# Expert stage of a fused kernel: five batches' rows scattered by expert and worked off in 95 tiles

## The reference, cut to what matters

```python
h = (x - mean) / sqrt(var + eps)
scores = sigmoid(h @ Wg.T)                       # 16 a row
choice = scores + bias                           # 4 groups of 4; the best 2 groups by
                                                 # the sum of their best two; then the best 4
w = scores[top4] / (sum(scores[top4]) + 1e-20) * 2.5
shared = relu2(h @ Ws1.T) @ Ws2.T                # 256 -> 256 -> 256, relu2(v) = relu(v)^2
x = x + shared + sum over the 4 chosen e of w_e * (relu2(h @ W1[e].T) @ W2[e].T)   # 256 -> 128 -> 256
```

## Time and profile before

| | us |
|---|---|
| median of 3 runs | 3248.0 (3244.1 to 3249.63) |
| the profiled execution | 3243.28 |
| its span, first to last instruction | 3241.4 |
| StageE, from its first load to the end of the span | 2688.0 to 3241.4 |

### The profile page before, as it was taken

One profiled execution on the slowest core, in us unless ns is written; L12 is line 12 of the kernel. 1 busy time (PEld: TensorE's weight loads), 2 busy tenths in 40 slices (PEclk: granted clock), 3 DMA queues, 4 the chain that ended last, 5 costly groups with the idle time before them and its releaser, 6 DMA issues.

```text
span 3241.4 us, 40482 instructions
## 1 busy us (share of the span) xinstructions
PE 2788.6 (86%) x13782; PEld 1680.9 (52%) x13782; DVE 2130.8 (66%) x3827; ACT 1629.6 (50%) x2433; POOL 1030.1 (32%) x715
## 2 busy tenths in 40 slices
PE   6878878887765799999969999968888988999999
PEld 3445544554443455555535666534444445666666
DVE  0688898888895677777522222246777785777776
ACT  2778778777861355555431111148877781111111
POOL 0888888888781221121010000011111000110000
PEclk9899999999867899999979999979999998999999
DMA  3577887788773775555432000010000002000000
GB/s 106 118 169 148 179 172 168 147 180 172 161 169 81 192 184 90 93 81 91 54 133 67 23 23 23 19 49 7 7 7 14 1 1 59 7 14 7 7 7 13
DMA packets 119272, 262.94 MB, mean 81 GB/s; under 512 B 14784, under 2 KB 72896, under 8 KB 117408
## 3 DMA queue, kind: packets, MB, share of 16 engines
q0 software_dynamic: 24928, 134.89, 20.0%
q1 hardware_dynamic: 94144, 125.47, 16.9%
HBM read 135.40 MB, written 131.20 MB: 82 GB/s over the span
## 4 chain that ended last, share of the span: by engine, by line
PE 50%; issue 6%; ACT 6%; DVE 5%; DMA 1%; SPq 0%; POOL 0%; POOLq 0%; ACTq 0%; DVEq 0%
PE PS L2345 7%; PE PS L1625 6%; PE PS L2363 6%; PE PS L1916 4%; PE PS L1647 3%; PE PS L1288 2%; PE PS L1966 2%; ACT Z L2074 2%; PE PS L1245 2%; PE PS L1267 2%; PE PS L1924 2%; PE PS L1270 2%; PE PS L1215 2%; PE PS L1984 1%; PE PS L1314 1%
## 5 line engine op out<-in xcount | busy, mean ns | idle before, releaser
L804 POOL TENSOR_TENSOR Z<-Z 128x1024 f32<-128x1024 f32 x256 | 648.4, 2761 | 45.8 <-DMA Z<-rows_b 40.9
L714 DVE TENSOR_TENSOR_SCAN Z<-PS,Z 128x1024 f32<-128x1024 f32 x256 | 576.5, 2276 | 18.4 <-POOL Z L804 13.6
L508 PE MATMUL PS<-Z 128*128 128x128 f32 x2048 | 305.1, 295 | 121.3 <-DVE Z L714 47.6
L508 PEld LDWEIGHTS PS<-Z 128*128 128x128 f32 x2048 | 250.7, 151 | 252.6 <-issue 81.7
L646 ACT ACTIVATE PS<-Z 128x511 f32<-128x511 f32 x512 | 332.8, 688 | 68.2 <-DVE Z L714 67.6
L1384 ACT ACTIVATE Z<-PS 128x512 f32<-128x512 f32 x320 | 188.9, 596 | 266.7 <-PE PS L1270 261.4
L2396 ACT ACTIVATE Z<-PS 128x512 f32<-128x512 f32 x144 | 85.9, 597 | 415.4 <-PE PS L2345 415.4
L2345 PE MATMUL PS<-Z 128*128 128x512 f32 x576 | 275.3, 604 | 7.9 <-DVE Z L2478 7.1
L658 ACT ACTIVATE Z<-PS,Z 128x512 f32<-128x512 f32 x378 | 246.0, 684 | 68.3 <-PE PS L508 61.5
L1477 DVE TENSOR_REDUCE Z<-PS 128x1 f32<-128x512 f32 (+2 forms) x384 | 182.8, 508 | 120.2 <-PE PS L1246 116.6
L2074 ACT ACTIVATE Z<-Z 128x2048 f32<-128x2048 f32 x128 | 252.4, 1996 | 12.9 <-PE PS L1966 9.3
(11 more groups left out here) (289 smaller groups left out, 4959.9 us busy)
## 6 DMA issues: line engine op xcount, KB each, us to landing
sums<-Z POOLq DMA_DIRECT2D x112, 768.0 KB, 8.4
Z<-rows_b SPq DMA_DIRECT2D x128, 256.0 KB, 4.6
Z<-scr SPq DMA_DIRECT2D x256, 128.0 KB, 7.2
rows_n<-in_L_ffn_expert_wv POOLq DMA_DIRECT2D x32, 528.0 KB, 7.7
scr<-Z SPq DMA_DIRECT2D x32, 384.0 KB, 3.5
Z<-Z POOLq DMA_DIRECT2D x14, 768.0 KB, 7.6
Z<-in_L_ffn_expert_wv SPq DMA_DIRECT2D x4, 2048.0 KB, 15.0
Z<-sums SPq DMA_DIRECT2D x7, 768.0 KB, 6.3
```

The costliest lines, as they stand in the source:

```text
L508: ins = e.transpose(self.turned[i % 2][:, c * 128:(c + 1) * 128], self.h(k, c // 2)[:, c % 2, i * 128:(i + 1) * 128], ident)
L714: e.tensor_tensor_scan(h, a, h, 0.0, ALU.mult, ALU.add).then_inc(s["scan"], 1)
L804: e.tensor_tensor(self.h(k, f), self.du[b % 2][:, 2 * f:2 * f + 2, :], b3(self.Bs[k % 2], 1, [128, 2, 512]), ALU.mult).then_inc(s["hin"], 1)
```

## The change

Batches 0 to 4 (`SP = 5`) no longer go through all experts. For each, DVE ranks the scores as before, POOL's part of it now on DVE too (`choice`), PE counts by matmuls with a triangular and an all-ones matrix how many rows before this one chose the same expert (`prefix`), DVE works out from that each row's four places (`place`), and POOL scatters the batch's normalised rows with 16 indirect DMAs of 128 rows (`rows_out`) into `rows_e`, a DRAM tensor with a region of 2,688 rows for each expert. That tensor is filled with finite numbers during StageD, by 32 DMAs from DRAM to DRAM on SP's queue, each behind a `yf` step. `slots` then works out, for each of 95 places (80 full tiles' worth of rows, and at most 15 more for the remainders of 16 experts), its expert and where it starts. Meanwhile PE does the shared expert and the first six experts (`FIRST = 6`) of batch 5.

Then come **95 tiles**: a gather of 128 rows (POOL), two transposes (`head`), a copy (ACT), the expert's number and two 128-column multiplications (`ups`), relu (ACT) and product (DVE), a transpose (`flips`) and a copy (DVE), one 256-column multiplication (`downs`), a copy (ACT) and a store to `rows_ye` (SP). Between them lie the preparation of batches 6 and 7 and `posy`, the places in `rows_ye`. Last, the ten remaining experts of batch 5 and batches 6 and 7 go through all experts as before; between their `down` steps, 20 `back` steps each gather four times 128 rows from `rows_ye` (POOL), and add them with their weights to x (DVE). The diff, cut to its core:

```diff
+        self.rows_e = m.nc.dram_tensor("rows_e", [StageE.NE * StageE.REG, 256], F32, kind="Internal").ap()
+        self.d_fill = m.lasting("d_fill_e")
...
+        n = StageE.NE * StageE.REG // StageE.FILLS
+        some = d["L0_ffn_expert_wv"].rearrange("x k m -> (x k m)")[0:n * 256].rearrange("(p n) -> p n", p=112)
+        for i in range(StageE.FILLS):
+            e.wait_ge(s["yf"], i + 1)
+            e.dma_start(self.rows_e[n * i:n * (i + 1)].rearrange("(p n) c -> p (n c)", p=112), some).then_inc(self.d_fill, 16)
...
+    SP, NE = 5, 16
+    NS = 16 * SP + NE - 1
+    REG = 128 * (4 * SP + 1)
+    FILLS = 32
+
+    FIRST = 6
...
+        def ahead(b):
+            return [("stats", b), ("rstd", b)], [("minus", b), ("norm", b), ("flip", b, 0), ("flip", b, 1), ("flipped", b),
+                                                 ("logits", b), ("exp", b)]
+
+        def shared(b):
+            return [("hidden", b, 0), ("hidden", b, 1)], [("down", b, 0, 0), ("down", b, 0, 1)]
+
+        def experts(b, xs):
+            out = []
+            for x in xs:
+                if x + 2 < 16:
+                    out.append(("hidden", b, x + 4))
+                out += [("down", b, 1 + x, 0), ("down", b, 1 + x, 1)]
+            return out
+
...
+        for b in range(2):
+            out += [s for part in ahead(b) for s in part]
+        for b in range(SP):
+            first, then = shared(b)
+            out += [("choice", b), *first, ("prefix", b)]
+            if b + 2 <= SP:
+                out += ahead(b + 2)[0]
+            out += [("place", b), ("rows_out", b)]
+            out += then
+            if b + 2 <= SP:
+                out += ahead(b + 2)[1]
+        first, then = shared(SP)
+        out += [("slots",), ("choice", SP), *first, ("hidden", SP, 2), *then, ("hidden", SP, 3)]
+        out += experts(SP, range(self.FIRST))
+        late = []
+        for b in range(SP + 1, NB):
+            late += ahead(b)[0] + ahead(b)[1] + [("choice", b)]
+        late = [("posy",)] + late
+        at = 0
+        out += [("head", 0), ("head", 1)]
+        for c in range(-1, NS + 1):
+            for what, i in (("ups", c + 1), ("rows", c + 4), ("head", c + 2), ("flips", c), ("downs", c - 1)):
+                if what == "head" and i < 2 or what == "rows" and i < 4:
+                    continue
+                if 0 <= i < NS:
+                    out.append((what, i))
+            upto = len(late) if c >= NS - 20 else len(late) * (c + 1) // (NS - 20)
+            out += late[at:upto]
+            at = upto
+        out += experts(SP, range(self.FIRST, 16))
+        for b in range(SP + 1, NB):
+            first, then = shared(b)
+            out += first + [("hidden", b, 2)] + then + [("hidden", b, 3)] + experts(b, range(16))
+
+        n = out.index(("down", SP, 1 + self.FIRST, 0))
+        downs = [i for i in range(n, len(out)) if out[i][0] == "down"]
+        every = max(1, len(downs) * 4 // 5 // (4 * SP))
+        where = {downs[every * g + 2]: g for g in range(4 * SP)}
+        full = []
+        for i, s in enumerate(out):
+            full.append(s)
+            if i in where:
+                b, k = divmod(where[i], 4)
+                full.append(("back", b, k))
+        return full
...
+        def head(c):
+            e.wait_ge(*self.d_gr.done(c))
+            if c >= 2:
+                e.wait_ge(s["hs"], c - 1)
+            else:
+                e.wait_ge(s["hid"], self.ups_before)
+            for k in range(2):
+                ins = e.transpose(self.hb[c % 2][:, k * 128:(k + 1) * 128], self.gr[c % 4][:, k * 128:(k + 1) * 128], ident)
+            ins.then_inc(s["ht"], 1)
+
+        def ups(c):
+            e.wait_ge(s["hs"], c + 1)
+            if c == 0:
+                e.wait_ge(s["slot"], 1)
+                e.wait_ge(s["acc"], self.dns_before)
+                for g in range(4):
+                    e.wait_ge(self.d_e[g], 32)
+            if c >= 2:
+                e.wait_ge(s["af"], c - 1)
+            expert[c] = e.value_load(self.esi[0:1, c:c + 1], min_val=0, max_val=self.NE - 1)
+            for k in range(2):
+                ins = e.matmul(self.ub[c % 2], self.hs[c % 2][:, k, :],
+                               self.w1f[:, bass.ds(expert[c] * 256 + 128 * k, 128)], start=k == 0, stop=k == 1)
+            ins.then_inc(s["tu"], 1)
+
+        def flips(c):
+            e.wait_ge(s["th"], c + 1)
+            e.transpose(self.tbk[c % 2], self.th[c % 2], ident).then_inc(s["flp"], 1)
+
+        def downs(c):
+            e.wait_ge(s["af"], c + 1)
+            if c >= 2:
+                e.wait_ge(s["y"], c - 1)
+            e.matmul(self.db[c % 2][:, 0:256], self.af[c % 2], self.w2f[:, bass.ds(expert[c] * 256, 256)],
+                     start=True, stop=True).then_inc(s["td"], 1)
+
...
+        def head(c):
+            e.wait_ge(s["ht"], c + 1)
+            if c >= 2:
+                e.wait_ge(s["tu"], c - 1)
+            e.activation(self.hs[c % 2].rearrange(FLAT), self.hb[c % 2][:, 0:256], ACT.Copy).then_inc(s["hs"], 1)
+
+        def ups(c):
+            e.wait_ge(s["tu"], c + 1)
+            if c >= 2:
+                e.wait_ge(s["th"], c - 1)
+            e.activation(self.tr[c % 2], self.ub[c % 2], ACT.Relu).then_inc(s["tr"], 1)
+
+        def downs(c):
+            e.wait_ge(s["td"], c + 1)
+            if c >= 3:
+                e.wait_ge(self.d_y[c % 3], 16 * (c // 3))
+            e.activation(self.yo[c % 3], self.db[c % 2][:, 0:256], ACT.Copy).then_inc(s["y"], 1)
+
...
+        def slots_(*_):
...
+            e.wait_ge(*own.now())
+            e.tensor_reduce(tiles, self.cmp, AX.X, ALU.add).then_inc(*own.tick())
+            for x in range(16):
                 e.wait_ge(*own.now())
-                e.reciprocal(sc, sc).then_inc(*own.tick())
+                e.tensor_tensor(tb[:, x + 1:x + 2], tb[:, x:x + 1], tiles[:, x:x + 1], ALU.add).then_inc(*own.tick())
+            e.wait_ge(*own.now())
+            shape = [128, NS, 15]
+            e.tensor_tensor(past, b3(slots, 2, shape), b3(tb[:, 1:16], 1, shape), ALU.is_ge).then_inc(*own.tick())
...
+            e.tensor_tensor(past, past, b3(tiles[:, 0:15], 1, shape), ALU.mult).then_inc(*own.tick())
+            e.wait_ge(*own.now())
+            e.tensor_reduce(loc, past, AX.X, ALU.add).then_inc(*own.tick())
+            e.tensor_copy(self.esi, es)
+            e.wait_ge(*own.now())
+            e.tensor_tensor(loc, slots, loc, ALU.subtract).then_inc(*own.tick())
+            e.wait_ge(*own.now())
+            e.tensor_scalar(loc, loc, float(4 * SP), 128.0, ALU.min, ALU.mult)
...
+        def ups(c):
+            e.wait_ge(s["tr"], c + 1)
+            if c >= 2:
+                e.wait_ge(s["flp"], c - 1)
+            e.tensor_tensor(self.th[c % 2], self.tr[c % 2], self.ub[c % 2], ALU.mult).then_inc(s["th"], 1)
+
+        def flips(c):
+            e.wait_ge(s["flp"], c + 1)
+            if c >= 2:
+                e.wait_ge(s["td"], c - 1)
+            e.tensor_copy(self.af[c % 2], self.tbk[c % 2]).then_inc(s["af"], 1)
+
+        def back(b, k):
+            for t in range(4):
+                g = 16 * b + 4 * k + t
+                e.wait_ge(self.d_gy[g % 8], 16 * (g // 8 + 1))
+                e.wait_ge(*((s["gat"], g - 3) if k else (s["acc"], self.n_dn[b, 0, t // 2] + 1)))
+                xx = m.X[:, 4 * b + t, :]
+                w = 16 * b + 4 * t + k
+                e.scalar_tensor_tensor(xx, self.gy[g % 8], self.wk[:, w:w + 1], xx, ALU.mult, ALU.add).then_inc(s["gat"], 1)
+
+        self.walk(stats=stats, minus=minus, choice=choice, place=place, slots=slots_, posy=posy, hidden=hidden, down=down,
+                  ups=ups, flips=flips, back=back)
...
+        def rows_out(b):
+            e.wait_ge(s["posi"], b + 1)
+            if b == 0:
+                e.wait_ge(self.d_fill, 16 * self.FILLS)
+            for t in range(4):
+                for k in range(4):
+                    c = 16 * b + 4 * t + k
+                    e.indirect_dma_start(self.rows_n, bass.IndirectOffsetOnAxis(ap=self.posi[:, c:c + 1], axis=0),
+                                         self.nt[b][:, t, :], None).then_inc(self.d_rows, 16)
+
+        def rows(c):
+            if c >= 4:
+                e.wait_ge(s["ht"], c - 3)
+            e.indirect_dma_start(self.gr[c % 4], None, self.rows_n,
+                                 bass.IndirectOffsetOnAxis(ap=self.start[:, c:c + 1], axis=0)).then_inc(*self.d_gr.over(c))
+
+        def head(c):
+            if c == 0:
+                e.wait_ge(s["slot"], 1)
+                e.wait_ge(self.d_rows, 256 * self.SP)
+                for i in range(4):
+                    rows(i)
+
+        def back(b, k):
+            if (b, k) == (0, 0):
+                e.wait_ge(s["posy"], 1)
+                for i in range(3):
+                    e.wait_ge(self.d_y[i], 16 * len(range(i, NS, 3)))
+            for t in range(4):
+                g, c = 16 * b + 4 * k + t, 16 * b + 4 * t + k
+                if g >= 8:
```

(88 more changed lines are left out.)

398 lines of the change are left out of this document (233 added, 165 removed).

## The result

The changed kernel takes 3321.3 us, median of 4 runs (3312.4 to 3340.1), against 3248.8 before (median of 4 runs, one more than above): ratio 1.0228, 95% interval 1.0200 to 1.0256. The forecast was 3301 us and slower; the time lies 20 us above it, inside its own range (3275 to 3325) and inside the wide one (3238 to 3352). It also lies nearer to the numbers of two rivals, 3334 for the half clock and 3324 for the bound by gathers, than to the forecast's.

The account below looks back on a forecast made before the run. PE was taken to bound StageE; seven steps summed to 606.2 us against 553.4, +52.8, giving span 3294.2 and median 3301 us, 1.6% slower. Its own range was 3275 to 3325, 8 in 10 3238 to 3352.

Parts of the forecast that it names:

- the half clock: Rival: PE's half clock holds through the tiles, 2.75 us a tile, 33 us more, 3334 us; chance 0.17.
- the bound by gathers: Rival: gathers of `back` become the bound, 4 x 1.57 us against 5.17, 23 us more, 3324 us; chance 0.09.
- Steps 1 to 4: StageE ahead of the tiles: first choice 13 us, five batches 108, `slots` and batch 5's choice 24.7, cover for scatters 32.
- a shared `down` at half clock: In the five batches: shared `down` at half clock outlasts DVE's moments and `place`, 1.6 us more a batch.
- Step 5: The 95 tiles: 228 us at 2.4 a tile, 32 for work put in between, 5 lead and drain; 265 us.
- The work put into the ring: In the tiles: two choices, `posy`, norms, flips and scores on DVE, and the clock after stalls; together 32 us.
- the ring: In the tiles: up product, relu, product, DVE's copy, then the load behind that wait; 2.32 us a turn, taken as 2.4.
- The faster rival: Load costs nothing or DVE's copy comes in time: tiles at 1.3 to 1.5 us, 90 us less, 3211 us; chance 0.16.
- Its deciding point: In the tiles: the rival of faster tiles decides from 1.85 us a tile down.
- Step 6: After the tiles, the rest through all experts: 155 us plus 4 for late first gathers, 159 us; returns barely fit.
- Step 7 and StageD: Last matmul to end 4.5 us, as now; fills in StageD 0, at most 5 if a gather is late.

Follow-up runs that it names:

- e5: Changed kernel plus four extra transposes a tile on PE, ahead of its `downs`, that nobody reads: 3340.0 us, ratio 1.0285.
- e12: Changed kernel with only the load of the expert's number moved ahead of both waits of the up product, on chip 3: 3282.9 us, ratio 1.0096.
- e10: Kernel of e8 without the 80 gathers of result rows and their 80 additions, on chip 3: 3223.3 us, ratio 0.9917.
- e4: Kernel before, with nothing of the change but its 32 fills in StageD: 3242.3 us, ratio 0.9985.
- e6: The changed kernel, unaltered, run again on chip 2: 3318.6 us, ratio 1.0215 to the kernel before.
- e7: Changed kernel with the load ahead of both waits of the up product and the flips' results in another bank: 3223.0 us, ratio 0.9921.
- e8: As e7, with the two late choices and `posy` cut into single instructions laid between tiles: 3205.8 us, ratio 0.9862.

## Why the prediction was right, and where it was 20 us off

Against the first profile after. StageE lasted 628.6 us where 606.2 were predicted.

The span missed by 30 us (3324.6 for 3294.2) and the median by 20. The 10 between are luck: the prediction put the median 4.7 us above the profiled execution, and it lay 5.1 below.

**Steps 1 to 4, ahead of the tiles.** Predicted 13 + 108 + 24.7 + 32 = 177.7; measured 12.1 + 102.1 + 23.6 + 31.0 = 168.8. The batch of choice and place took about 20.4 and not 21.65: the 20.05 of DVE's sum were right, and the 1.6 for a shared `down` at half clock were largely not needed, although the clock did fall (0.75 over the stretch). (By the prediction's own numbers, 6.9 - 4.75, it would have been 2.1.) DVE sets this part, at 128 of 168 us busy. The scatters lay under steps 3 and 4, as said.

**Step 5, the tiles: the term that was mis-sized.** Predicted 265, measured 288.1. The mechanism held piece by piece: relu 0.28 (0.27), product 0.20 to the copy, copy 0.28, 0.91 from copy to product (0.05 + 0.85), together 2.45 for 2.32. The difference is nearly all PE's: from the up product's start to the relu's 0.75 us for 0.64. The work put into the ring cost 30 us for 32. Missing was the clock. 45% of the tile stage passed at half clock, where a turn takes 3.11 us, 0.66 longer and not 0.4; I had seen that risk, made it a rival at 0.17, and took 2.4 for the mean. Without the holes the mean was 2.70, nearer to that rival's 2.75. e5 prices the clock at 17 us, three quarters of the 23; most of the rest is the ring's 0.05 above 2.4, 5 us.

**The faster rival** supposed that a tile could cost 1.45. In the kernel as it stands the tiles are 2.45 apart, so it is out. Its deciding point, 1.85 us a tile, was nearly right: e12 with 1.82 has tiles 73 to 75 us shorter than the changed kernel's, and the changed kernel is 69 to 73 us behind the one before. e12's own ratio, 1.010, has chip 3's losses in it.

**Step 6.** Predicted 159, measured 167.3. Steady steps kept to the old pace: with returns among them three experts' `hidden` lie 10.3 us apart, 3 x 3.44 as in the earlier trace rows. The gathers did not become the bound. POOL's groups in the changed kernel, gathers of tiles and of returns:

```profile
L2852 POOL DMA_INDIRECT Z<-rows_e,Z x95 | 90.5, 953 | 211.7 <-PE PS L2518 204.7 <-issue 3.9 <-DMA rows_e<-Z 3.2
...
L2871 POOL DMA_INDIRECT Z<-rows_ye,Z x80 | 81.8, 1023 | 45.5 <-DMA rows_ye<-Z 16.8 <-issue 16.8 <-DVE Z L2826 11.9
```

A return's gather takes 0.07 us more than a tile's, 5.6 us in all. By the rule of the Trainium skill ("SBUF — State Buffer", "SBUF: two separate sides") that the prediction weighed, it would have been up to some 30. What was missed is the change of batch: there DVE owes PE hidden products at once, and four additions with their waits for gathers stand ahead of them (3.0 of PE's 4.4 idle us at 3259.68). By e10, and across chips, all of the returns cost 8.5 us where I had 4.

**Step 7 and StageD.** 4.4 for 4.5. The fills were put at 0, and e4 confirms it. StageE began 8 us later than before in the first profile after, 3.7 in e6 and 1 earlier in e7: a spread between executions, not a cost.

The sum: -9 ahead, +23 in the tiles, +8 behind, and of the 8 at the start most is spread.

## What to carry to other kernels

A read of a register in a sequencer sits where it stands in the list: put it ahead of *every* wait of the step, since one wait left in front of it makes the next ring (2.45, 2.15, then 1.82 us a tile; 1.65 with the other bank). Where each turn of a pipeline must pass an engine, give that engine's side work to it in pieces no longer than its slack; the same instructions as blocks cost 17 us (e8). And work that is taken from the bounding engine is gained only as far as the ring that remains is shorter than the work was: 160 us of PE's columns were at stake here, and the change lost 70 until the load stood elsewhere and a result lay in another bank (e7).

## What was not expected of the hardware

- PE given 4 unused transposes more a tile finished 95 tiles 17 us sooner, at a granted clock of 0.94 in place of 0.78.
- On two of three chips, waits on semaphores ended late while POOL issued indirect DMAs back to back: 20 to 25 us over 80 scatters and 10 to 20 over 80 returns, with DVE's waits for its own results at 0.5 to 1.2 us. The kernel before, with few such DMAs at a time, took the same time on all three (3247 to 3250 us). Whether it is the chip or the session is open; a comparison of kernels of this kind holds within one of them only.
- Over twelve profiles of identical code, StageE's start lay between 2687 and 2698 us.
